# Two GroupNorm convolution blocks on one core: transfers of two units at a time, bands read in row order, and a new order of the work

## What is computed

```
x = x + L0(gn(x))     # L0: depthwise, alpha0*v + alpha1*conv1x1 + alpha2*conv3x3 + alpha3*conv5x5, weights per channel
x = x + L1(gn(x))     # L1: one shared 3x3 kernel plus one bias, on every channel
```

## Time and profile before

| | |
|---|---|
| Runs: median (lowest to highest) | 478.0 us (477.63 to 478.91), n = 3 |
| Profiled execution: its own time, its span | 481.88 us, 480.1 us |
| TensorE matmul, weight load | 328.6 us (68%), 270.3 us (56%) |
| VectorE | 341.8 us (71%) |
| ScalarE | 305.1 us (64%) |
| GpSimd | 274.5 us (57%) |
| Mean granted clock of TensorE | 0.884 of full |
| DMA queue of SyncE, of ScalarE | 55.2%, 2.9% of 16 engines' span |
| Bytes moved | 73.82 MB, 154 GB/s |

### The profile page before, as it was taken

One profiled execution on the slowest core, in us unless ns is written; L12 is line 12 of the kernel. 1 busy time (PEld: TensorE's weight loads), 2 busy tenths in 40 slices (PEclk: granted clock), 3 DMA queues, 4 the chain that ended last, 5 costly groups with the idle time before them and its releaser, 6 DMA issues.

```text
span 480.1 us, 12659 instructions
## 1 busy us (share of the span) xinstructions
PE 328.6 (68%) x5176; PEld 270.3 (56%) x5176; DVE 341.8 (71%) x740; ACT 305.1 (64%) x373; POOL 274.5 (57%) x196
## 2 busy tenths in 40 slices
PE   2055093987678867879695979758958796965740
PEld 2044093977547745656574666637846585952520
DVE  7396977769787677958595768777687957586510
ACT  0133284778785867685878778784877867828421
POOL 3041455657674766575767657673776766627512
PEclk9999576999979978988989798979999999996975
DMA  8955354635867485848567674768384616150554
GB/s 183 226 120 149 93 138 133 137 106 143 199 184 196 128 197 147 213 138 219 146 189 192 180 201 136 196 196 204 101 218 138 161 59 168 37 148 2 151 145 135
DMA packets 116178, 73.82 MB, mean 154 GB/s; under 512 B 6903, under 2 KB 111479, under 8 KB 116120
## 3 DMA queue, kind: packets, MB, share of 16 engines
q1 hardware_dynamic: 109496, 69.86, 55.2%
q10 hardware_dynamic: 6624, 3.15, 2.9%
HBM read 46.35 MB, written 31.89 MB: 163 GB/s over the span
## 4 chain that ended last, share of the span: by engine, by line
PE 23%; DVE 22%; SPq 17%; DMA 15%; ACT 10%; issue 6%; POOL 3%; ACTq 1%; POOLq 0%; DVEq 0%
PE ps L335 22%; DVE stats L570 10%; DVE xt L625 8%; SPq L242 8%; DMA tap_scratch<-edge_scratch 5%; ACT cross L501 4%; ACT gn_fY L491 3%; DMA haloX<-tap_scratch 3%; ACT gnY L492 3%; POOL gnY L809 3%; DMA edge_scratch<-gnX 2%; SPq L236 2%; SPq L218 2%; SPq L194 2%; DMA haloY<-tap_scratch 1%
## 5 line engine op out<-in xcount | busy, mean ns | idle before, releaser
L335 PE MATMUL ps<-gnX,band 64*64 64x512 f16 x2880 | 191.1, 412 | 12.3 <-ACT gnX L492 12.3
L625 DVE SCALAR_TENSOR_TENSOR xt<-ps,unscale,xt 128x512 f32<-128x512 f32 (+1 forms) x192 | 142.2, 747 | 61.8 <-PE ps L335 60.0
L335 PEld LDWEIGHTS ps<-gnX,band 64*64 64x64 f16 x2880 | 158.6, 190 | 35.9 <-issue 27.0
L809 POOL TENSOR_TENSOR gnX<-gn_fX,gnX 128x768 f16<-128x768 f32 x60 | 92.6, 1543 | 62.1 <-ACT gnX L492 62.1
L570 DVE BATCH_NORM_STATS2 stats<-xt 128x6 f32<-128x384 f32 x256 | 122.4, 546 | 2.4 <-DMA xt<-in_x_dram 1.4
L335 PE MATMUL ps<-gnY,band 64*64 64x512 f16 x1728 | 116.5, 414 | 10.8 <-ACT gnY L492 5.6
L501 ACT ACTIVATE cross<-ps,unscale 64x512 f32<-64x512 f32 x96 | 65.5, 682 | 82.5 <-PE ps L335 81.3
L809 POOL TENSOR_TENSOR gnY<-gn_fY,gnY 128x768 f16<-128x768 f32 x60 | 92.6, 1543 | 33.7 <-ACT gnY L492 33.7
L335 PEld LDWEIGHTS ps<-gnY,band 64*64 64x64 f16 x1728 | 92.6, 190 | 25.3 <-ACT gnY L492 6.2
L818 POOL TENSOR_TENSOR xt<-xt,cross 128x512 f32<-128x512 f32 x48 | 61.2, 1275 | 78.5 <-ACT cross L501 77.4
L491 ACT ACTIVATE gn_fX<-xt,g_add,g_mul 128x768 f32<-128x768 f32 x60 | 61.0, 1017 | 27.6 <-DVE g_add L614 27.6
(11 more groups left out here) (82 smaller groups left out, 136.6 us busy)
## 6 DMA issues: line engine op xcount, KB each, us to landing
out_dram<-xt SPq DMA_DIRECT2D x124, 192.0 KB, 3.0
xt<-in_x_dram SPq DMA_DIRECT2D x116, 192.0 KB, 3.9
band_raw<-diag_scratch SPq DMA_DIRECT2D x32, 240.0 KB, 3.9
tap_scratch<-edge_scratch SPq DMA_DIRECT2D x16, 246.9 KB, 3.3
haloX<-tap_scratch SPq DMA_DIRECT2D x32, 123.4 KB
xt<-in_x_dram ACTq DMA_DIRECT2D x12, 192.0 KB, 6.3
haloX<-tap_scratch SPq DMA_DIRECT2D x32, 61.7 KB
tap_scratch<-edge_scratch SPq DMA_DIRECT2D x16, 74.1 KB
```

Of the source, the lines that this page charges most:

```text
L335: mm = nc.tensor.matmul(ps[to, c, half, :], weights(rows, half), moving(rows, half), start=first, stop=last)
L625: ev = nc.vector.scalar_tensor_tensor(out=here, in0=ps[frm, c, half, :].rearrange("h (b w) -> h b w", b=NB), scalar=unscale[rows, at:at + ...
L809: nc.gpsimd.tensor_tensor(gn_lo[s][:, i % 2, :, b, :, PAD:PAD + W].rearrange("p e c w -> p c e w"), gn_f[s][:, k % NF, :, :, :], gn_hi[s][ ...
```

## The change

Loads and stores handle two units together. `xt` has 4 slots of two units, and channels are mapped to units so that a group's two units are 6 neighbouring channels (weights are loaded in the matching order):

```diff
-    NX = 6
-    NF = 4
+    NX = 4
+    NF = 2
+    WIN = 8
+    RUN = (R + R // WIN - 1) * NM
-        xt = sb("xt", [P, NX, NB, CG, 2, W])
-        gn_f = [sb(f"gn_f{s}", [P, NF, CG, 2, W]) for s in "XY"]
+        xt = sb("xt", [P, NX, NB, 2, CG, 2, W])
+        gn_f = sb("gn_f", [P, 2 * NF, CG, 2, W])
+        def first_channel(i, g):
+            return 4 * CG * (i // 2) + 2 * CG * g + CG * (i % 2)
+        def load_pair(eng, m, b):
+            for g in range(2):
+                c = first_channel(2 * m, g)
+                eng.dma_start(xt[HALVES[g], m % NX, b, :, :, :, :].rearrange("p u c e w -> p (u c e) w"),
+                              x[b, c:c + 2 * CG, :, :].rearrange("c (e p) w -> p (c e) w", e=2)).then_inc(x_in[m % NX], 16)
```

Bands come from a table of 8 shifted runs for each channel, which the start writes; `load_band` is three DMAs, one for a channel, straight into `band5` in the right order. The flips on VectorE and GpSimd and `band_raw` are gone:

```diff
-        def flip(eng, k):
+            def load_band(i):
+                if i >= 2:
+                    sp.wait_ge(conv_done[X], 4 * CG * (i - 1))
+                for c in range(CG):
+                    k = 4 * CG * (i // 2) + 2 * (CG * (i % 2) + c)
+                    win = diag_dram[k:k + 1, :, :]
+                    sp.dma_start(band5[:, i % 2, c, :],
+                                 bass.AP(win.tensor, win.offset + (R // WIN - 1) * NM,
+                                         [[RUN, 2 * WIN], [-NM, R // WIN], [1, R * NM]])).then_inc(band_in[i % 2], 16)
```

SyncE's turn; odd turns load a pair, even turns store one:

```diff
+            def in_and_out(j, batches):
+                m = (j + 3) // 2 if j % 2 else j // 2 - LAG
+                for b in batches:
+                    if j % 2 and 2 <= m < NU // 2:
+                        if m >= NX:
+                            sp.wait_ge(stored[m % NX], 128 * (m // NX))
+                        load_pair(sp, m, b)
+                    elif j % 2 == 0 and m >= 0:
+                        unit_ready(2 * m + 1)
+                        store_pair(sp, m, b)
+                    elif j == PERIODS - 1:
+                        unit_ready(LAST - 1)
+                        store_unit(sp, LAST - 1, b)
             for j in range(PERIODS):
                 y = j - LAG
+                if 1 <= j < NU:
+                    edges_in(sp, X, j)
+                if 1 <= j < LAST:
+                    load_band(j + 1)
                 if y >= 0:
                     edges_out(sp, Y, y)
-                if j < NU:
-                    store_part(j - 3, (0, 1))
+                in_and_out(j, (0,))
                 if y >= 0:
                     edges_spread(sp, Y, y)
-                if j < NU:
-                    store_part(j - 3, (2, 3))
+                in_and_out(j, (1, 2))
                 if y >= 0:
                     edges_in(sp, Y, y)
...
                 if j + 1 < NU:
                     edges_out(sp, X, j + 1)
-                load_part(j + 3, (2,))
+                in_and_out(j, (3,))
                 if j + 1 < NU:
                     edges_spread(sp, X, j + 1)
-                load_part(j + 3, (3,))
-                if j + 1 < NU:
-                    edges_in(sp, X, j + 1)
```

TensorE's turn. The statistics of normalisation i+1 now stand inside X(i)'s first channel, ahead of its parts 5 and 12 of 15:

```diff
+                    if statistics is not None and n == 5:
+                        mean_product(statistics)
+                    if statistics is not None and n == 12:
+                        var_product(statistics)
...
                 elif i < NU:
-                    for c in range(CG):
-                        whole(X, i, c)
+                    conv(X, i, 0, None, i + 1)
+                    conv(X, i, 1)
+                    edge(X, i, 0)
+                    edge(X, i, 1)
+                    conv(X, i, 2)
+                    edge(X, i, 2)
```

ScalarE's turn: the crossing of Y's third channel moves to the next turn, behind root; batches and crossings of Y alternate in other sizes:

```diff
                 root(j + 1)
+                if y >= 1:
+                    cross_over(y - 1, 2)
                 if j + 1 < NU:
                     normalize(X, j + 1, j + 1, 0)
-                normalize(Y, j - 1, j + 1, NB, (0,) if j < NU else range(NB), j < NU)
-                if y >= 0:
+                normalize(Y, j - 1, j + 1, NB, (0, 1), j < NU)
+                if y >= 0 and j < NU:
                     cross_over(y, 0)
-                if j < NU:
-                    normalize(Y, j - 1, j + 1, NB, (1, 2))
+                normalize(Y, j - 1, j + 1, NB, (2, 3), j < NU)
+                if j == NU:
+                    cross_over(y, 0)
                 if y >= 0:
                     cross_over(y, 1)
-                    cross_over(y, 2)
```

VectorE's turn, and its small operations. mean, dev and r0 become SBUF tiles, `stats` gets two buffers, and the normalisation has 7 counted steps instead of 9:

```diff
             for i in range(PERIODS):
+                if i > LAG:
+                    evacuate(Y, i - LAG - 1, 1)
+                    evacuate(Y, i - LAG - 1, 2)
                 if 1 <= i <= NU:
+                    deviations(i + 1)
+                    if i + 2 < NU:
+                        x_stats(i + 2, 0)
+                        x_stats(i + 2, 1)
                     affine(i + 1)
+                    if i + 2 < NU:
+                        x_stats(i + 2, 2)
+                        x_stats(i + 2, 3)
...
+                    for c in range(CG):
+                        evacuate(X, i, c)
                 if i >= LAG:
                     evacuate(Y, i - LAG, 0)
-                    if i < NU:
-                        deviations(i + 2)
-                    evacuate(Y, i - LAG, 1)
-                    evacuate(Y, i - LAG, 2)
-                elif i < NU:
-                    deviations(i + 2)
+                if i < NU:
+                    y_stats(i)
```

```diff
-                nc.vector.tensor_scalar(var_eps[:, :], var[:, :], GN_EPS, None, ALU.add).then_inc(var_read, 1)
-                nc.vector.tensor_tensor(newton[:, :], r0, var_eps[:, :], ALU.mult).then_inc(norm_step, 1)
+                nc.vector.scalar_tensor_tensor(out=newton[:, :], in0=var[:, :], scalar=GN_EPS, in1=r0[:, :],
+                                               op0=ALU.add, op1=ALU.mult).then_inc(norm_step, 1)
-                nc.vector.tensor_tensor(newton[:, :], r0, newton[:, :], ALU.mult).then_inc(norm_step, 1)
-                nc.vector.tensor_scalar(newton[:, :], newton[:, :], -0.5 * G_SCALE, 1.5 * G_SCALE, ALU.mult, ALU.add)\
-                  .then_inc(norm_step, 1)
+                nc.vector.scalar_tensor_tensor(out=newton[:, :], in0=newton[:, :], scalar=-0.5 * G_SCALE, in1=r0[:, :],
+                                               op0=ALU.mult, op1=ALU.mult).then_inc(norm_step, 1)
-                nc.vector.tensor_tensor(g_mul[:, n % 2, :], r0, newton[:, :], ALU.mult).then_inc(norm_step, 1)
+                nc.vector.scalar_tensor_tensor(out=g_mul[:, n % 2, :], in0=newton[:, :], scalar=1.5 * G_SCALE, in1=r0[:, :],
+                                               op0=ALU.add, op1=ALU.mult).then_inc(norm_step, 1)
```

295 lines of the change are left out of this document (129 added, 166 removed).

## The result

The changed kernel takes **483.0 us** (median of 6 runs, 482.32 to 484.92) against 478.36 for the kernel before on the same chip: ratio 1.010, interval 1.007 to 1.012. It is 1% slower, where 446 was forecast, and lies outside the range of 414 to 466.

What follows compares the result with a forecast made beforehand. No engine is full; waits for statistics and halos, with SyncE's issue queue in the cycle, bound the kernel. Steady turns -29.7, start -4.6, tail +2, together -32.3 from 481.9: 449.6, scaled to 446 us; range 414 to 466.

Steps and rivals of the forecast that it cites:

- Pairs, 5.4 us off SyncE: SyncE's queue: 8 bulk issues a period in place of 16, at 0.67 us each, save 5.4 us.
- Halo Y behind the bulk: SyncE's queue: halo Y stands behind 2.36 MB and lands 12.8 us after the first bulk transfer, upper bound 14.4.
- T: Zero of the forecast's period schedule, in us: where convolution X(i) begins on TensorE.
- Storing turns: Even periods: first store at T+9.7, halo Y at T+22.5, wanted at 17.7, 4.8 late; period 25.0 us.
- 0.4 a period: VectorE: cost of six small operations now reading two SBUF tiles, each bounded between 0 and 1.54 us.
- Loading turns: Odd periods: first load at T+5.9, halo Y at 18.7, 21.1 us; with 0.4 of the norm 21.5.
- Start: Before the steady turns: statistics of unit 2 would end about 4.6 us earlier, bounds 0 and 7.
- Tail: After the last statistics: halo Y of units 14 and 15 held up in SyncE's queue, +2 us, bounds -3 and +8.
- hidden by 0.7 only: X's halo, fetched at the head of the next period: landed by T+8.3, wanted at T+9.0, so no wait.
- The fourth: Rival: halo X late too, 460 us, or a pair's issue costs double, queue not relieved, 455; together chance 0.12.
- the third: Rival: six two-SBUF VectorE operations each wait about 0.5 to 0.7 us; VectorE 22.6 a period, about 458; chance 0.13.
- the fifth: Rival: each of the six operations waits a whole GpSimd operation, 1.54 us; VectorE 28.4 a period, about 515; chance 0.05.

Runs made afterwards that it cites:

- PSUM run: Kernel after the change with mean, deviations and reciprocal back in PSUM, one more operation for the deviations: 473.7 us, ratio 0.987.
- order runs: Kernel after with all halo Y hops ahead of bulk: 494.3 us; with two batches ahead instead of three: 468.6; the latter plus a semaphore per batch: 451.6.
- start run: Kernel after with unit 2 alone loaded before X(0)'s edges and unit 3 after them, in place of one pair batch: 476.7 us, ratio 0.992.
- tail run: Kernel after with all three hops of Y's halo ahead of the last stores in the last two turns: 474.6 us, ratio 0.989.

## Why the prediction was wrong, step by step

**Pairs, 5.4 us off SyncE.** The run with pairs issued as single units shows nothing gained. An issue of 0.67 was right for the first transfers of a block (1.34 for two). Behind them four took 5.07 and a copy 2.10: 2.36 MB in 10.1 us from the first store on is 234 GB/s, near the 256 of the earlier trace rows, and issued in halves the same bytes took 10.6. So the step counted issuing and moving as two costs where one covers the other.

**Halo Y behind the bulk** was the right mechanism, and in storing turns its size was right: 12.7 to 13.2 from the first store to the edge product (12.8). That the first store also goes at T+9.6 (forecast 9.7; T is 228.07 there) is luck: T itself came 4.3 after the Y edge before it, where the forecast had 2.55, since the 36 products there ran at a low clock (3.72 us for 2.09). Measured from that edge, which leaves T out, the first store comes after 13.8 to 14.0 in five of the storing turns; the forecast's terms give 2.55 + 9.7 = 12.25. Turns without bulk came out at 20.8 as forecast, so the unhindered period was right as well. What was wrong was the time round it.

**Storing turns, 25.0 for 26.7 (+1.7, six times).** The step that failed is the price of the two-operand operations: "0.4 a period", with the deviations counted at 0.7 with the mean. Not even the 0.4 is in the 25.0, though the deviations stand ahead of the first store (T+22.5 and the 2.55 behind it make 25.05). From the Y edge (250.61) VectorE has the deviations ready for the variance product at 259.52, 8.9 us later; the forecast's terms gave 4.7 + 1.5 + 0.7 = 6.9. The two operations account for 1.8 of the 2.0. This chain carries root, crossing, addition and the first store, so it shifts halo Y of the turn. In the PSUM run the first store comes 12.4 to 13.0 after the edge, and the storing turns are 1.1 shorter in the mean (1.6 in the one shown): that confirms most of it. The affine, whose lock was priced the same way, met none (0.17). The Trainium skill (SBUF — State Buffer, section SBUF: two separate sides) names VectorE operations with two SBUF inputs as locked out by a GpSimd operation that reads SBUF; the runs agree for the deviations, and 5.41 us show more than the one instruction of GpSimd's that the forecast took as a whole: several in a row were waited out.

**Loading turns, 21.5 for 24.75 (+3.25, five times): the largest error.** The step that failed is "the first load goes at T+5.9 and halo Y lands at 18.7": it let only GpSimd's low parts gate the load, counted from TensorE's T. In fact GpSimd's last low part of Y ended at 258.18, 2.1 before SyncE sent the Y edges (260.28), and nothing but SyncE's issues and the landings it waits for is in this chain: from the first store (237.65) to halo Y of the loading turn (275.34) it takes 37.7 us, and the forecast's terms give 25.0 - 9.7 + 18.7 = 34.0. After halo Y has landed (250.6) come X's spread behind the last batch of stores, 5.0 us until it has landed, halo X and the band, and the first load goes 10.9 after the landing, where the forecast's terms make it 8.5; halo Y then lands 13.9 after it, not 12.8, a figure taken from a turn of stores. In the five loading turns it is 10.1 to 10.8 and 13.9 to 14.7. Halo Y was therefore 3.5 to 3.6 us late for TensorE in the loading turns shown, where the forecast had 1.0. (18.7 and the 2.55 behind it make 21.25; the forecast wrote 21.1, which changes nothing.) The forecast asked which engine gates each transfer, turn by turn; it never added up the queue over one storing and one loading turn. The order runs show the same from the other side: two batches ahead of halo Y, the last one behind X's spread, and a semaphore for each batch are worth 31 us, and bring the loading turns to 21.8. Which of these shifts does it wasn't tried apart. Nor do the runs tell whether the halos are late because their queue works in order or because the transfer engines are shared: with the stores on GpSimd's queue small copies on SyncE's were slow too (6.2 us for 2.5).

**Start (+5.5).** Forecast: 4.6 earlier, bounds 0 and 7. TensorE did begin earlier (25.01 for 27.76), but the eight pair loads kept X(0)'s edges back until 49.47. The 3.1 MB were named and then not priced; the start run returns 6.3 us by moving half of them: Y's statistics of unit 2 begin at 91.16 there, where the forecast had 91.9.

**Tail (+5.2 where +2 was forecast, bound +8)**: halo Y of unit 14, behind 2.36 MB, cost 10.30 us of idleness, and the last one came at 464.98. The tail run returns 8.4.

**Halo X "hidden by 0.7 only"** held in the steady turns; its one long wait is that of the start. **The clock** was a consequence, as forecast.

**The rivals.** None had this. The fourth had the right place in its second half, a queue not relieved, but let it end at 455, and the third and the fifth the right mechanism for the lock, of which 0.98 and 1.20 in two operations of six came true. The sign was wrong because +1.7, +3.25, +5.5 and +3.2 all lay on one side: each is a part of the same queue or of the chain that feeds it, and they were priced as if they were independent. The Trainium skill (DMA: Bandwidth & Descriptors, section Bandwidth) advises to batch into transfers of 1 MiB or more; the step from 192 to 384 KB had nothing to give here, since halving them again cost nothing, and no run has a transfer of 1 MiB.

## What to carry to other kernels

When small latency-bound copies share a queue with bulk transfers, write down that queue's whole cycle, every issue and every landing that the issuer waits for, over as many turns as the pattern has; its sum is a bound like an engine's, and here it was not moved by issuing less often. Look for gains in what stands ahead of what, one batch at a time, with a semaphore for each piece that is used by itself: taking everything out from ahead of one halo only made the other one late. Merging loads of two units and stores of two units into alternate turns is not itself the loss: spreading the bytes over all turns, with fewer of them ahead of halo Y, was 38 us faster than the change, but with the order and the semaphores put right, the new start, the last turns and PSUM operands the pairs reached 429.1 us, and the single units, with the same start and PSUM operands, 438.6.
